# One place fewer for reloaded strips, one more for input strips, and channel sums half a unit earlier

## The chip, the cores and the metric

The kernel runs on one core of one Trainium2 chip. A core has TensorE (PE), VectorE (DVE), ScalarE (ACT), GpSimd (POOL) and SyncE (SP, which here only issues DMAs), an on-chip memory SBUF with 128 partitions, the accumulators in PSUM, and 16 DMA engines to HBM. The metric is the device time of one execution in microseconds (us); lower is better.

## The reference

The input x has 16 images of 112 x 112 pixels with 256 channels in float32. What is computed, cut to what matters:

```python
x  = x + conv3x3_depthwise(sign(groupnorm(x)), sign(kernel))     # x1
v  = groupnorm(x)
gate = sigmoid(fc(mean(v)) + fc(max(v)))                         # per image and channel
xc = v * gate
m, mx = mean(xc, channels), max(xc, channels)                    # two feature maps
y  = state_space_scan(m)                                         # along the pixels, 16 states
s  = conv7x7(concat(m, mx))
x2 = xc * sigmoid(y) + xc * sigmoid(s)
out = x + relu(batchnorm(x2))
```

The channel gate of an image needs the sums of the whole x1 of that image, so the feature maps of an image can only be made once its convolution is done, and the scan and the batch norm need all images.

## The kernel before

The kernel has three stages: (1) a loop over the 16 images that makes x1, the gates and the feature maps; (2) the scan, the 7 x 7 convolution and the sums of the batch norm, with x1 read again; (3) a last pass that reads x1 once more and writes the output. The change is in stage 1 and in the hand-over to stage 2.

**Half steps.** An image is cut into 7 units of 8 rows in each half of the image, and a unit into its two groups of 128 channels. One pair (unit, group) is a half step, h = 0 to 13. In half step h of image i TensorE convolves (18 matmuls with `taps`, L1338), turns, from half step 2 on, two tiles of the next image from pixels to channels on the partitions (`turn_tile`, L1244, 7 transposes each, the first in the midst of the convolution, the second at the end of the half step; the last four of the 28 tiles follow half step 13), and works on two strips of the image before: `channel_sums` (L1277, 16 matmuls, the sum over the channels of a gated strip) and `blocks_back` (L1291, 7 transposes of the maximum over the two channel groups). ScalarE brings turned tiles to SBUF (`evacuate`, L750), converts the convolution (`pack`, L758), brings the channel sums to SBUF (`average`, L813), squares (`square`, L766), and gates a strip (`apply_gate`, L795 and L799: both channel groups for the strips 0, 1 and 10 to 13; for strips 2 to 9 only the first, and VectorE does the second in `gate_half`, L1107). VectorE makes the signs (L961, L976), takes the maximum of the two groups (`max_halves`, L1117), reduces the turned blocks (L1128), and adds the convolution to x (`add_convolution`, L1022, L1028).

**Strips.** The feature maps of image i - 1 are made while image i is convolved. Its x1 is read back from HBM in 14 strips of 896 pixels. `strip_at(i, h, lag)` gives the strip that is `lag` half steps behind: in half step h, SP loads strip h - 1 (`load_g`, L576 to L585), ScalarE gates strip h - 3, VectorE takes the maximum of strip h - 4, TensorE sums and turns back strip h - 5, and ScalarE averages strip h - 5. Below zero these are the last strips of the image before that. Strip 9 of image i - 1 would fall to half step 0 of the next image; it is handled at the end of image i instead: `blocks_back(i - 1, 9)`, a wait for all tiles of the next image, `channel_sums(i - 1, 9)`, and only then `group_sums` (L1250), the matmul on whose result the mean of the next image (L951) and all its signs wait.

**Places.** Reloaded strips go round a ring of four places `xg` (the halves of the two tiles `xc`); `load_g` waits until the strip four before has been summed and its maximum taken. Input strips x go round three places `xin` in `stage`; each load (L569) waits until the tiles of the strip three before have been turned. Sums over channels stand in PSUM in `turn[c % 2]`, the two accumulators that the convolution also uses in turn, so the convolution of half step h waits (`averaged`, L1334) until the sum that was made in the other use of its accumulator has been brought out.

**Averaged sums.** ScalarE writes two strips each into a row buffer `srow[s % 2]`, s = c // 2, and SP stores the pair to HBM (`sums_out`, L594). An image has seven pairs, so its last pair (s = 6) and the first pair of the next image (s = 0) use the same buffer, and `average` of strip 0 waits until the store of pair 6 has landed:

```python
def average(i, c):
    s, b = c // 2, c // 2 % 2
    act.wait_ge(summed, i * NP + c + 1)
    if c % 2 == 0:
        act.wait_ge(sum_out[b], i * (16 * turns(b, 2, NS)) + 16 * (s // 2) + 1)
```

**SP's order.** SP issues everything from one queue, in the order written. In half step h: the next x strip, the store of x1 of half step h - 1 (L589), `load_g` of strip h - 1, then in even half steps `sums_out` of the pair of strip h - 6 (pair 6 in half step 4), then the row of maxima (L599). A wait in one of them holds all that follow.

Before image 0 its x strips are loaded and turned (L569, L1244); then 42 tiny loads of parameters follow on SP (L612, L615), a store of `bands`, and then the first three x strips of image 1. In image 15 there is no next image; TensorE computes part of the 7 x 7 convolution (`spatial`, L556) in its place, for which SP loads features (L440) in half step 3.

Of the kernel before, what the change touches and what calls it, by code (L numbers as in the profile page):

```python
# [5 lines left out]
def binary_conv_then_gated_ssm_block(  # L6
# [74 lines left out]
    with ctx:  # L81
# [6 lines left out]
        def sem(name):  # L88
# [8 lines left out]
        xin = [stage[:, b * SP:(b + 1) * SP].rearrange("p (t c) -> p t c", c=C) for b in range(3)]  # L97
        picks = stage[0:12, 3 * SP:3 * SP + 4 * P]
# [3 lines left out]
            "p (j n) -> p j n", j=NJ) for b in range(4)]  # L102
# [133 lines left out]
        x_in = [sem(f"x_in{b}") for b in range(3)]  # L236
# [30 lines left out]
        g_in = [sem(f"g_in{b}") for b in range(4)]  # L267
# [17 lines left out]
        def sum_ps(c):  # L285

            return turn[c % 2][:, 0:SQ]
# [7 lines left out]
        def ring(i, c):  # L295
            return (i * NP + c) % 4

        def ring_turns(i, c):

            return (i * NP + c) // 4 + 1  # L300
# [262 lines left out]
        with nc.Block() as block:  # L563
            @block.sync
            def _(sp):
                def load_x(i, k):
                    p = pair(k)
                    p0, p1 = unit_px(p // 2, p % 2)
                    sp.dma_start(xin[k % 3], x_strips[i, p0:p1, :].rearrange("(p t) c -> p t c", t=TG)  # L569
                                 ).then_inc(x_in[k % 3], 16)  # L570

                def load_next_x(i, k):
                    sp.wait_ge(turned, i * NTILE + 2 * (k - 3) + 2)
                    load_x(i, k)

                def load_g(i, c):  # L576
# [63 lines left out]
                def image(i):  # L640
                    more = i + 1 < NB
                    if more:
                        sp.wait_ge(turned, i * NTILE + NTILE)
                        for p in range(3):
# [90 lines left out]
            def _(act):  # L735
# [48 lines left out]
                def apply_gate(i, c, resident=False):  # L784
# [4 lines left out]
                    if resident:  # L789
                        act.wait_ge(maxed, i * NP + c - 3)  # L790
                        act.wait_ge(summed, i * NP + c - 3)
# [26 lines left out]
                def image(i):  # L818
                    first, more, channels = i == 0, i + 1 < NB, i >= 1
                    for h in range(NP):  # L820
# [8 lines left out]
                        if (at := strip_at(i, h, 5)) and h >= 1:  # L829
# [21 lines left out]
                    if more and channels:  # L851
                        average(i - 1, 9)
# [10 lines left out]
                average(NB - 2, 9)  # L863
# [356 lines left out]
            def _(pe):  # L1220
                pe.wait_ge(consts_made, 14)

                def turn_tile(i, n):
# [3 lines left out]
                    b = k % 3  # L1227
                    if j == 0:
                        pe.wait_ge(x_in[b], i * (16 * turns(b, 3, NP)) + 16 * (k // 3 + 1))
# [641 lines left out]
```

## Time and profile before

| what | value |
|---|---|
| median of 3 runs | 3481.12 us (3471.48 to 3544.35) |
| the profiled execution | 3476.38 us |
| its span in the trace | 3474.7 us |
| mean granted TensorE clock, as a share of full speed | 0.832 |
| busy: PE, DVE, ACT, POOL | 2596.4, 3053.3, 2693.6, 19.9 us |
| DMA traffic | 1227.99 MB, 353 GB/s over the span |

Stage 1 runs to about 1775 us after the span's start (the last convolution matmul starts at 1772.6 us), stage 2 to about 2485 us, the last pass to the end. All times below are from the start of the span. An arrow in a row names what ended the idle time before the instruction.

### The profile page before, as it was taken

What the parts mean: (1) busy time and instruction counts of PE and PEld (TensorE: products, weight loads), DVE (VectorE), ACT (ScalarE), POOL (GpSimd) and SP (SyncE); (2) the same over time, 40 slices, a digit from 0 to 9 for tenths busy, and PEclk for the clock granted to TensorE, in tenths of its full rate; (3) what the DMA queues carried; (4) which work ended last, traced back from release to release, by engine and by line L of the source; (5) the groups of instructions that cost most, each with busy time, mean ns of one, the idle gap of its engine ahead of it and who ended that gap; (6) DMA issues with size and microseconds to landing.
All of it is one profiled execution on the core that took longest, in us unless ns stands there. A gap on an engine that the chain in (4) does not pass through costs nothing. (4 is left out here: it accounts for less than half of the span.)

```text
span 3474.7 us, 50996 instructions
## 1 busy us (share of the span) xinstructions
PE 2596.4 (75%) x17105; PEld 1661.0 (48%) x17105; DVE 3053.3 (88%) x4395; ACT 2693.6 (78%) x3748; POOL 19.9 (1%) x23
## 2 busy tenths in 40 slices
PE   4899999999999998999877333333377767777676
PEld 3565555655556555566443010000255555555555
DVE  5689989999999998999886599999898899899997
ACT  3788887878888888888674287777788888888887
POOL 1000000000000000000000000000000000000000
PEclk8999999999999999999998555555577787777777
DMA  5898888988889888898765399999499999999998
GB/s 177 316 406 346 352 340 355 396 343 351 350 353 404 350 347 344 350 405 346 254 205 133 87 414 416 416 416 414 198 423 427 427 418 418 419 419 421 420 421 340
DMA packets 258888, 1227.99 MB, mean 353 GB/s; under 512 B 36421, under 2 KB 45537, under 8 KB 244353
## 3 DMA queue, kind: packets, MB, share of 16 engines
q1 hardware_dynamic: 258688, 1225.40, 89.0%
q8 instruction: 117, 1.92, 0.2%
q14 instruction: 83, 0.67, 0.1%
HBM read 805.14 MB, written 420.17 MB: 353 GB/s over the span
## 5 line engine op out<-in xcount | busy, mean ns | idle before, releaser
L1338 PE MATMUL psum<-signs,taps 128*128 128x448 f16 x4032 | 876.6, 362 | 49.1 <-DVE signs L976 44.9
L1759 PE MATMUL psum<-ident,xt 128*128 128x128 f32 x3136 | 560.5, 348 | 281.0 <-ACT stage L1793 232.5
L1759 PEld LDWEIGHTS psum<-ident,xt 128*128 128x128 f32 x3136 | 498.7, 212 | 367.2 <-ACT stage L1793 309.2
L1439 PE MATMUL psum<-signs,picked 12*128 12x448 bf16 x896 | 328.8, 510 | 356.1 <-DMA signs<-gate_scratch 287.3
L1338 PEld LDWEIGHTS psum<-signs,taps 128*128 128x128 f16 x4032 | 395.3, 100 | 381.0 <-issue 48.1
L1793 ACT ACTIVATE stage<-psum 128x512 f32<-128x512 f32 x784 | 407.1, 612 | 173.7 <-DMA out_dram<-stage 149.4
L1814 DVE SCALAR_TENSOR_TENSOR xc<-xt,curs,psum 128x1792 f32<-128x1792 f32 x224 | 456.1, 2077 | 85.7 <-PE psum L1439 81.2
L750 ACT ACTIVATE xt<-psum 128x896 f32<-128x896 f32 x416 | 377.9, 912 | 162.9 <-PE psum L1244 162.7
L1623 DVE SCALAR_TENSOR_TENSOR xc<-xt,curs,psum 128x1792 f32<-128x1792 f32 x224 | 455.6, 2078 | 49.5 <-PE psum L1439 34.4
L1244 PE MATMUL psum<-ident,stage 128*128 128x128 f32 x3136 | 416.5, 277 | 76.6 <-DMA stage<-x_dram 43.7
L1561 ACT ACTIVATE xc<-xc 128x1792 f32<-128x1792 f32 x224 | 380.1, 1697 | 113.6 <-DVE xc L1623 113.6
L1829 DVE TENSOR_TENSOR xt<-xc,xt 128x1792 f32<-128x1792 f32 x224 | 442.6, 2018 | 0.0
L1028 DVE CUSTOM_DVE_ANT_0 xt<-scratch,xt 128x896 f32<-128x896 int8 (+1 forms) x416 | 436.1, 1085 | 0.0
L1244 PEld LDWEIGHTS psum<-ident,stage 128*128 128x128 f32 x3136 | 364.9, 143 | 118.7 <-DMA stage<-x_dram 50.2
L1781 ACT ACTIVATE xc<-xc,bn,curs 128x1792 f32<-128x1792 f32 x224 | 411.3, 1900 | 8.6 <-DVE xc L1814 8.4
L766 ACT ACTIVATE hsum<-xt,nmean 128x1792 bf16<-128x1792 f32 x208 | 370.4, 1781 | 0.7
L1439 PEld LDWEIGHTS psum<-signs,picked 12*128 12x128 bf16 x896 | 86.7, 117 | 562.5 <-DVE xc L1623 380.1
L1128 DVE TENSOR_REDUCE pmax<-psum 128x4 f32<-128x512 f32 x448 | 257.7, 617 | 73.3 <-PE psum L1291 73.2
L758 ACT ACTIVATE scratch<-psum,border 128x896 int16<-128x896 f32 x224 | 223.9, 1000 | 82.8 <-PE psum L1338 82.4
L1117 DVE TENSOR_TENSOR stage<-xc 128x896 f32<-128x896 f32 x224 | 243.9, 1089 | 27.4 <-ACT xc L795 19.5
L976 DVE SCALAR_TENSOR_TENSOR signs<-xt,mean,signs 128x896 f16<-128x896 f32 x208 | 240.3, 1155 | 7.4
L1291 PE MATMUL psum<-ident,stage 128*128 128x128 f32 x1568 | 223.8, 282 | 24.1 <-ACT pmax_rows L806 13.8
(199 smaller groups left out, 2205.9 us busy)
## 6 DMA issues: line engine op xcount, KB each, us to landing
xt<-x_scratch SPq DMA_DIRECT2D x210, 1792.0 KB
stage<-x_dram SPq DMA_DIRECT2D x224, 896.0 KB, 9.0
out_dram<-stage SPq DMA_DIRECT2D x112, 1792.0 KB, 13.7
xc<-x_scratch SPq DMA_DIRECT2D x210, 896.0 KB, 8.3
x_scratch<-xt SPq DMA_DIRECT2D x208, 896.0 KB, 7.5
x_scratch<-last_unit SPq DMA_DIRECT2D x16, 896.0 KB, 6.9
signs<-ssm_scratch SPq DMA_DIRECT2D x28, 448.0 KB, 4.6
signs<-gate_scratch SPq DMA_DIRECT2D x217, 10.5 KB
```

What stands on the lines that cost most here:

```text
L750: nc.scalar.activation(dst, src, ACT.Identity, scale=PACK if part else 1.0, accum_out=xsum_p[:, j, 2 * u + part:2 * u + part + 1]).then_in ...
L1028: nc.vector.tensor_tensor_reduce(out=px, in0=conv, in1=px, scale=1.0 / PACK if part else 1.0, scalar=-3.0e38, op0=ALU.add, op1=ALU.max, ac ...
L1244: ins = nc.tensor.transpose(ring[:, t * P:(t + 1) * P], xin[b][:, t, j * P:(j + 1) * P], ident[:, :])
L1338: return nc.tensor.matmul(turn[h % 2][:, b * 512:b * 512 + HB], taps[:, j, t, :], signs[:, j, r:r + RT // 2, dw:dw + W], start=t == 0, sto ...
L1439: last = nc.tensor.matmul(dst[:, b, :], picked[:, b * P:(b + 1) * P], gate_rows[:, s * BW:(s + 1) * BW], start=True, stop=True)
L1561: nc.scalar.activation(u, u, ACT.Square, accum_out=g2_p[:, n, j, bass.ds(it, 1)]).then_inc(squared3, 1)
L1623: nc.vector.scalar_tensor_tensor(fours(xc[n % 2][:, j, :]), fours(slots[s][:, j, :]), curs[:, h, j:j + 1], gate_ps3[n % 2], ALU.add, ALU.mult,
L1759: last = nc.tensor.transpose(out_ps[k % 4][:, v * C + j * P:v * C + (j + 1) * P], block_in, ident[:, :])
L1781: nc.scalar.activation(u, u, ACT.Relu, bias=bn[:, 7, j:j + 1], scale=curs[:, h, NJ + j:NJ + j + 1]).then_inc(relu_made, 1)
L1793: nc.scalar.activation(outs[n % 2][:, 2 * k:2 * k + 2, :].rearrange("p t c -> p (t c)"), out_ps[k % 4], ACT.Identity).then_inc(staged, 1)
L1814: nc.vector.scalar_tensor_tensor(fours(xc[n % 2][:, j, :]), fours(slots[s][:, j, :]), curs[:, h, j:j + 1], gate_ps4, ALU.add, ALU.mult).th ...
L1829: nc.vector.tensor_tensor(x1, u, x1, ALU.add).then_inc(x2_made, 1)
```

## The change

It does the following:

- The ring `xg` has three places instead of four; `load_g` waits for the strip three before.
- The free place becomes a fourth place of `xin`. An x load waits for the turn of the strip four before, and each strip is loaded one half step earlier: strip 0 of the next image in half step 13 of the image before (for image 1: right behind the x loads of image 0 and ahead of the parameter loads), strips 1 to 3 at the start of an image.
- `channel_sums` and `average` go from five half steps behind to four. `blocks_back` stays at five. The half step 0 now has sums (of strip 10), the special case at the end of an image keeps only `blocks_back(i - 1, 9)`, and `sum_ps` changes its parity so that the sums still lie in the accumulator that is not being convolved into.
- The convolution's wait for `averaged` and the wait of the third last turned tile are moved by one strip to match.
- The call of `sums_out` in SP's program is as before.

```diff
         def sum_ps(c):
-            return turn[c % 2][:, 0:SQ]
+            return turn[(c + 1) % 2][:, 0:SQ]
...
                 def load_x(i, k):
...
+                    b = (i * NP + k) % NX
...
                 def load_next_x(i, k):
-                    sp.wait_ge(turned, i * NTILE + 2 * (k - 3) + 2)
+                    sp.wait_ge(turned, i * NTILE + 2 * (k - NX) + 2)
...
-                    if i * NP + c >= 4:
-                        sp.wait_ge(maxed, i * NP + c - 3)
-                        sp.wait_ge(summed, i * NP + c - 3)
+                    if i * NP + c >= 3:
+                        sp.wait_ge(maxed, i * NP + c - 2)
+                        sp.wait_ge(summed, i * NP + c - 2)
...
-                for p in range(3, NP):
+                for p in range(NX, NP):
                     load_next_x(0, p)
+                load_next_x(1, 0)
...
                     if more:
-                        sp.wait_ge(turned, i * NTILE + NTILE)
-                        for p in range(3):
-                            load_x(i + 1, p)
+                        for p in range(1, NX):
+                            load_next_x(i + 1, p)
                     for h in range(NP):
-                        if h >= 3 and more:
-                            load_next_x(i + 1, h)
+                        if h >= NX - 1 and more and (i + 2 < NB or h < NP - 1):
+                            load_next_x(i + 1 + (h + 1) // NP, (h + 1) % NP)
...
-                        if (at := strip_at(i, h, 5)) and h >= 1:
+                        if at := strip_at(i, h, 4):
                             average(*at)
...
-                        if strip_at(i, h, 6):
-                            pe.wait_ge(averaged, (i - 1) * NP + h - 5)
+                        if strip_at(i, h, 5):
+                            pe.wait_ge(averaged, (i - 1) * NP + h - 4)
...
-                        if (at := strip_at(i, h, 5)) and h >= 1:
+                        if at := strip_at(i, h, 4):
                             pe.wait_ge(unpack_in, i * NP + h)
                             channel_sums(*at)
+                        if (at := strip_at(i, h, 5)) and h >= 1:
                             blocks_back(*at)
...
                             blocks_back(i - 1, 9)
-                            pe.wait_ge(evacuated, (i + 2) * NTILE)
-                            channel_sums(i - 1, 9)
                         group_sums(i + 1)
```

## Rows read from the trace of the kernel before

**Rows 1.** The page, the chain that ended last, share of the span by line
```profile
DMA out_dram<-stage 20%; ACT stage L1793 3%; PE psum L1759 2%; DVE xc L1814 1%; DVE xt L1829 1%; PE psum L1439 0%; ACTq L1792 0%; ACT xc L1781 0%; SPq L1722 0%; ACTq L1712 0%; ACTq L1779 0%; ACTq L1790 0%; ACTq L1798 0%; DVEq L1812 0%; DVEq L1810 0%
```
**Rows 2.** Windows: window, us, busy (instructions) of each engine, clock, DMA share, GB/s
```profile
918.10:1024.90 106.80, 99.20 (x789) 63.83 (x788) 98.61 (x203) 88.77 (x139) 0.00 (x0) 0.98 0.92 362
```
**Rows 3.** Timeline of PE, one image, half steps 3 to 5: start, us, instruction
```profile
1043.50 0.96 PE L1277 MATMUL psum<-xc,over_c 128*32 128x224 f32 x16
...
1050.78 0.96 PE L1277 MATMUL psum<-xc,over_c 128*32 128x224 f32 x16
...
1053.37 2.07 PE L1338 MATMUL psum<-signs,taps 128*128 128x448 f16 x10
...
1060.38 0.55 PE L1291 MATMUL psum<-ident,stage 128*128 128x128 f32 x3 [1.06 <-ACT pmax_rows L806]
```
**Rows 4.** Timeline of ACT, same stretch
```profile
1043.19 1.12 ACT L799 ACTIVATE xc<-xc,gbias,cur 128x896 f32<-128x896 f32 x1
...
1050.07 1.12 ACT L799 ACTIVATE xc<-xc,gbias,cur 128x896 f32<-128x896 f32 x1
...
1052.88 0.35 ACT L813 ACTIVATE hsum<-psum 128x224 f32<-128x224 f32 x1
...
1060.51 0.36 ACT L813 ACTIVATE hsum<-psum 128x224 f32<-128x224 f32 x1 [0.18 <-DMA feat_scratch<-hsum]
```
**Rows 5.** Timeline of DVE, half step 4: the maximum of strip 0
```profile
1054.63 1.09 DVE L1117 TENSOR_TENSOR stage<-xc 128x896 f32<-128x896 f32 x1
```
**Rows 6.** Timeline of SP's DMA issues, half step 4
```profile
1053.64 0.49 SPq L584 DMA_DIRECT2D xc<-x_scratch  x1
1054.18 0.91 SPq L594 DMA_DIRECT2D feat_scratch<-hsum  x1
```
**Rows 7.** The same store one image later, its waiter, and all DMAs of that tensor
```profile
1161.55 0.90 SPq L594 DMA_DIRECT2D feat_scratch<-hsum  x1
...
1169.54 0.36 ACT L813 ACTIVATE hsum<-psum 128x224 f32<-128x224 f32 x1 [1.51 <-DMA feat_scratch<-hsum]
...
DMA to landing us min/median/max: 3.5/6.1/9.6
```
**Rows 8.** Timeline of PE in image 0, from half step 2 on
```profile
87.23 1.75 PE L1244 MATMUL psum<-ident,stage 128*128 128x128 f32 x7 [11.72 <-DMA stage<-x_dram]
...
95.03 0.93 PE L1244 MATMUL psum<-ident,stage 128*128 128x128 f32 x7
...
99.99 0.27 PE L1244 MATMUL psum<-ident,stage 128*128 128x128 f32 x1
```
**Rows 9.** Waits of PE from 200 to 2000 us, and timelines at two image ends
```profile
PE psum L1244 <- DMA stage<-x_dram: 18.8, 12, 2.4
...
683.39 2.46 PE L1244 MATMUL psum<-ident,stage 128*128 128x128 f32 x21
...
692.80 0.16 DVE L951 TENSOR_SCALAR mean<-psum 128x2 f32<-128x2 f32 x1 [0.47 <-PE psum L1250]
...
1223.48 2.46 PE L1244 MATMUL psum<-ident,stage 128*128 128x128 f32 x21
...
1231.21 0.16 DVE L951 TENSOR_SCALAR mean<-psum 128x2 f32<-128x2 f32 x1 [0.96 <-PE psum L1250]
```
**Rows 10.** Timeline of SP's DMA issues before image 0
```profile
48.92 7.03 SPq L612 DMA_DIRECT2D scol<-A_dram  x8
...
78.84 3.02 SPq L569 DMA_DIRECT2D stage<-x_dram  x3
```
**Rows 11.** PE's sums in half step 10, DVE's gating of the strip in half step 9
```profile
985.70 0.96 PE L1277 MATMUL psum<-xc,over_c 128*32 128x224 f32 x16
...
986.12 0.75 DVE L1107 TENSOR_SCALAR xc<-xc,cur,gbias 128x896 f32<-128x896 f32 x1
```
**Rows 12.** Image 15: the feature loads on SP, and PE's wait for them
```profile
1694.12 3.15 SPq L440 DMA_DIRECT2D stage<-feat_scratch  x2
...
1705.04 4.79 PE L556 MATMUL psum<-stage 112*112 112x448 f32 x6 [4.46 <-DMA stage<-feat_scratch]
```

More of the change, by code:

```diff
@@ L97, in binary_conv_then_gated_ssm_block @@
         xin = [stage[:, b * SP:(b + 1) * SP].rearrange("p (t c) -> p t c", c=C) for b in range(3)]
+        NX = 4
         picks = stage[0:12, 3 * SP:3 * SP + 4 * P]
@@ L101, in binary_conv_then_gated_ssm_block @@
         xg = [xc[b // 2][:, :, :].rearrange("p j n -> p (j n)")[:, b % 2 * SP:(b % 2 + 1) * SP].rearrange(
-            "p (j n) -> p j n", j=NJ) for b in range(4)]
+            "p (j n) -> p j n", j=NJ) for b in range(3)]
+        xin.append(xc[1][:, :, :].rearrange("p j n -> p (j n)")[:, SP:2 * SP].rearrange("p (t c) -> p t c", c=C))
         bands0 = xc[0][0:H, :, :].rearrange("p j n -> p (j n)")[:, 0:KS * 2 * H].rearrange(
@@ L235, in binary_conv_then_gated_ssm_block @@
         taps_made = sem("taps_made")
-        x_in = [sem(f"x_in{b}") for b in range(3)]
+        x_in = [sem(f"x_in{b}") for b in range(NX)]
         turned = sem("turned")
@@ L266, in binary_conv_then_gated_ssm_block @@
         gate_in = sem("gate_in")
-        g_in = [sem(f"g_in{b}") for b in range(4)]
+        g_in = [sem(f"g_in{b}") for b in range(3)]
         gated = sem("gated")
@@ L295, in ring @@
         def ring(i, c):
-            return (i * NP + c) % 4
+            return (i * NP + c) % 3
         def ring_turns(i, c):
-            return (i * NP + c) // 4 + 1
+            return (i * NP + c) // 3 + 1
         def tile(n):
@@ L603, in _ @@
                     sp.dma_start(dst[:], src).then_inc(params_in, 16)
-                for p in range(3):
+                for p in range(NX):
                     load_x(0, p)
                 sp.dma_start(lsa[:, :], lsa_d.broadcast_to([H, KS * KS * 2])).then_inc(lsa_in, 16)
-                for p in range(3, NP):
+                for p in range(NX, NP):
                     load_next_x(0, p)
+                load_next_x(1, 0)
                 for src, col in ((A_d[0, :], 0), (B_w_d[:, 0], 1), (B_b_d, 2), (C_w_d[:, 0], 3), (C_b_d, 4)):
@@ L789, in apply_gate @@
                     if resident:
-                        act.wait_ge(maxed, i * NP + c - 3)
-                        act.wait_ge(summed, i * NP + c - 3)
+                        act.wait_ge(maxed, i * NP + c - 2)
+                        act.wait_ge(summed, i * NP + c - 2)
                     else:
@@ L850, in image @@
                     square(i, NU - 1, 1, first)
-                    if more and channels:
-                        average(i - 1, 9)
                     inverse_deviation(i)
@@ L862, in _ @@
                 apply_gate(NB - 2, 11)
-                average(NB - 2, 9)
                 gate_exp(NB - 1)
@@ L1226, in turn_tile @@
                     k = (2 * u + part + 2) % NP
-                    b = k % 3
+                    b = (i * NP + k) % NX
                     if j == 0:
-                        pe.wait_ge(x_in[b], i * (16 * turns(b, 3, NP)) + 16 * (k // 3 + 1))
+                        pe.wait_ge(x_in[b], 16 * ((i * NP + k) // NX + 1))
                     if i == 0:
@@ L1236, in turn_tile @@
                         if i >= 2:
-                            pe.wait_ge(averaged, (i - 2) * NP + 9)
+                            pe.wait_ge(averaged, (i - 2) * NP + 10)
                     elif n >= NTILE - 2:
@@ L1393, in _ @@
                 hidden(NB - 1)
-                channels_late(NB - 2, 9)
+                blocks_back(NB - 2, 9)
                 gate(NB - 1)
```

5 lines of the change are left out of this document (2 added, 3 removed).

## The prediction

> **What bounds the kernel now.** I read the page's chain first. The end of the span is a last pass whose time is DMA stores [rows 1]; its length doesn't depend on stage 1, so what stage 1 gains or loses passes to the end in full. Next the windows, one for each image: an image of stage 1 takes about 107 us, in which TensorE is busy for 99.2, VectorE for 98.6 and the DMA engines for 0.92 of the time [rows 2]. No engine has room; a wait of a microsecond anywhere is likely to be seen, fourteen times over. So I read the timelines of one image, engine by engine, to see who sets the pace where. From mean to half step 2 it is VectorE; from there on TensorE, with ScalarE close behind it in half steps 2 to 5, where it gates both channel groups and still has its two tiles and its squares.
>
> **The change, part by part.** All times are those of the image in [rows 3 to 6]; "old" is the trace, "new" my walk through the new order.
>
> *Sums one half step nearer to the gating.* In half step 3 TensorE comes to its sums at 1043.50 [rows 3]. Before, that was strip 12, gated long ago. Now it is strip 13, whose second gating ends at 1043.19 + 1.12 = 1044.3 [rows 4]: 0.9 late. The blocks, the second tile and ScalarE's move of it follow, so ScalarE's next gating (strip 0) ends not at 1050.07 + 1.12 = 1051.2 but at 1052.1, and the sums of strip 0 in half step 4 start at 1052.2 instead of 1050.78 [rows 3, 4]: 1.4 late. By itself this costs about 1.4 us an image; in the later half steps the gating ends some tenths before the sums. Half step 10 is the other tight one: sums at 985.70, VectorE's gating of that strip ends at 986.12 + 0.75 = 986.9 [rows 11], 1.2 late. VectorE doesn't wait for TensorE in between, so this is not added to the 1.4 but covered by it.
>
> *The average of strip 0.* This is the large term. `average` of strip 0 may not write its row buffer before the store of the last pair of the image before has landed. Old, that store was issued at 1054.18 in half step 4 [rows 6], and the average came one half step later: it started at 1060.51, after a wait of 0.18 us for just this store [rows 4]. One image on it is 1161.55 and 1169.54, with a wait of 1.51 [rows 7]. So landing takes 6.3 to 8.0 us where ScalarE waited, and there was no slack to give away. New, the average stands in half step 4, where ScalarE comes to it at about the old 1052.88 + 1 = 1053.8 [rows 4], while SP still issues the store in half step 4. And SP comes to it later than before: ahead of it in the queue stands `load_g` of strip 3, which with three places waits for the maximum of strip 0 (four places: of the last strip of the image before). That maximum ends at 1054.63 + 1.09 = 1055.7 [rows 5]. Load and store are 0.54 us apart [rows 6], so the store is issued at 1056.3 and, with 6.4 us, lands at 1062.7. ScalarE stands still for 8.9 us, and all that is queued behind it there: a tile, the squares, the gating of strip 1. TensorE's convolution of half step 5 needs the accumulator that holds the sum, so it starts at 1063.2 instead of 1053.37 [rows 3]: 9.8 late.
>
> *TensorE's clock.* It then has idled for 8 us. The nearest row is image 0: after 11.72 us of idle time seven transposes took 1.75 us instead of 0.93, the half rate, and from there to the same place of the next half step it took 95.03 - 87.23 = 7.8 us where the next one takes 99.99 - 95.03 = 5.0 [rows 8]. I take 2.8 us. Back goes the wait of 1.06 us for the row of maxima in half step 5 [rows 3], since ScalarE will have done that row while TensorE is slow. Sum: 9.8 + 2.8 - 1.0 = 11.6 us an image, the 1.4 included (it runs beside the wait for the store). VectorE is held about as long, since its maximum of strip 1 waits for the gating behind the average; so the tight place in half step 10 stays covered. From below: the shortest landing of that tensor is 3.5 us [rows 7], and with no slow clock ScalarE's own order sets the restart, about 7 us. From above: 8.0 us of landing gives 13.2, the longest landing, 9.6, gives 14.8.
>
> It holds for images 2 to 14, 13 x 11.6 = 151 us. In image 1 strip 0 is the first of all and nothing is waited for; 0.9 for the gating. In image 15 the store waits in the same way; the feature loads behind `load_g` in half step 3 come some 3 us later than 1694.12, but TensorE, which idled 4.46 us for them [rows 12], now idles for the average instead. There the slow clock is already in the old time, and half step 10 costs its 1.2 again, since TensorE is slower than VectorE there: about 10.4. Stage 2 begins with a reload that waits for strip 10 instead of 9; I put it at nothing within 2 us.
>
> *The image's end.* The sums of strip 9 stood ahead of the group sums; without their 0.9 us the mean comes 0.5 us earlier (ScalarE's last tile and VectorE's sum of it are then what is late), 14 x 0.5 = 7. The fourth x place brings the last x strip one half step earlier, so the waits for it go: 12 waits, 18.8 us [rows 9]. Not all of it was paid: from the start of the last tiles to the mean it takes 1231.21 - 1223.48 = 7.7 us where there was no such wait, and 692.80 - 683.39 = 9.4 with one of 2.4 [rows 9]. ScalarE, which moves the tiles one by one, hid 0.7 to 0.9 of each. 18.8 - 12 x 0.9 = 8. Together -15 us.
>
> *The start.* Strip 0 of image 1 was loaded behind 42 parameter loads that occupy SP from 48.92 on, at 78.84 [rows 10], and TensorE idled 11.72 us until 87.23 [rows 8]. Now it stands ahead of them, and half step 2 runs without a wait. Half step 3 then waits for strip 1, still behind the parameters. These start earlier by as much as the fourth place speeds up the loads of image 0, which I put at 6 us (3 to 9: one strip is there at the start, and four transfers are under way instead of three). So x is issued near 73 and lands 8.4 us later (87.23 - 78.84), at 81.3; with TensorE slow again for 2.8 us that is like 84.1 at full rate, against 95.03: -11 us (-5 to -13).
>
> The sum: 151 + 10.4 + 0.9 - 15 - 11 = +136. The profiled execution took 3476.4 us (1.7 outside its span), so 3612; the median of the runs is 5 us above it, less than what I can tell.
>
> A rule of the Trainium skill speaks to the largest term. DMA: Bandwidth & Descriptors, section Anatomy of one DMA, gives a transfer a fixed part of about 2 us, most of it the confirmation of the write, and these stores have 7 KB each. By that the store would have landed 2 us after its issue, the old trace would show no wait, and the sum would be near 3550 (an estimate from that page's figure). The trace doesn't agree where it counts: 6.3 and 8.0 us [rows 4, 6, 7], right behind a reload of 896 KB.
>
> **The rivals.**
>
> *The store lands soon.* The landings of that tensor go down to 3.5 us [rows 7]. In the new order TensorE is held up each time, so the DMA engines may have less before the store. Against it: the reload issued 0.54 us ahead of it is the same. With 3.5 us and little of the slow clock, 7 us an image: 13 x 7 + 5.8 + 0.9 - 26 = +72, 3548.
>
> *It lands late.* 9.6 us [rows 7] gives 14.8 an image: 13 x 14.8 + 13.6 + 0.9 - 26 = +181, 3657.
>
> *Not slower: the average isn't held.* This is so if the store has landed before 1053.8, thus was issued by 1047.5, that is in half step 3, ahead of the load of strip 3. What speaks for it is that its data, the average of strip 13, is ready at 1046.4. Against it is the order of SP's program. Then an image pays only 1.4: 13 x 1.4 + 0.9 + 4.6 (image 15: 3.4 for the features behind `load_g`, and half step 10) - 26 = -2, 3474. The same holds if the fourth x place is what counts and I have misread the wait.
>
> **How the numbers follow.** The forecast, landing in 6 to 8 us, has 0.62; soon 0.17; late 0.11; not held 0.10. The likeliest gives 3612. The range leaves out the case "not held" and the tail of "late": 3540 to 3650. A measurement of this kernel can tell about 2%, 70 us. The not-held case and half of the soon case lie within it, 0.18; slower by more 0.81; faster by more 0.01, since all that is gained is 26 us.
>
> **What would show it right or wrong.** Right: in images 2 to 15 ScalarE waits some 8 to 9 us ahead of L813 in half step 4, ended by the store to `feat_scratch`, 14 times, where it was 0.2 and 1.5 us in the rows shown; SP issues that store just behind a reload that waited for VectorE's maximum; L1338 waits 8 us for L813, with slow matmuls behind it; an image takes near 117 us; no PE wait for x at an image's end; TensorE's wait in image 0 shorter and one half step later. Wrong: if the wait at L813 is under 4 us (landing), or absent and images still near 107 us. If images are longer than 120 us, the reload's longer wait also starves a gating, which I hold unlikely: it is issued 2 us later than before and has two half steps, 13 us, to land.

## The result, and the profile after

The changed kernel takes 3627.4 us (median of four runs, 3602.5 to 3652.1) where the kernel before takes 3476.3 in the same comparison: ratio 1.044, 95% interval 1.037 to 1.051. It is slower, as forecast; 3612 had been predicted, with a range of 3540 to 3650. Two of the four runs took 3602 and 3604 us, the other two 3650 and 3652. The profiled execution is one of the longer two: it took 3650.3, its span is 3648.6.

First the sum of waits. The page's group of the convolution and two rows of the waits, from 200 to 2100 us (engine, line, releaser: us in total, times, longest):

```profile
L1338 PE MATMUL psum<-signs,taps 128*128 128x448 f16 x4032 | 900.7, 369 | 172.2 <-ACT hsum L816 129.1
```
```profile
ACT hsum L816 <- DMA feat_scratch<-hsum: 120.8, 15, 13.7
PE psum L1338 <- ACT hsum L816: 128.9, 28, 12.6
```

L816 is `average`. ScalarE stood before it for 120.8 us in all, until a store of the sums had landed: 7.5 to 9.5 us in each of the images 2 to 14, 13.7 in image 15 and 0.5 once behind it. TensorE stood before its convolution for 128.9 us, until ScalarE had made that average. Then one image, the one with its mean at 1066.29, in half steps 3 to 5. SP's DMA issues (to hold against [rows 6]), VectorE's maximum [rows 5], ScalarE [rows 4] and TensorE [rows 3]:

```profile
1104.16 0.55 SPq L592 DMA_DIRECT2D x_scratch<-xt  x1
1107.07 0.37 SPq L587 DMA_DIRECT2D xc<-x_scratch  x1
1107.48 0.73 SPq L597 DMA_DIRECT2D feat_scratch<-hsum  x1
```
```profile
1105.85 1.09 DVE L1117 TENSOR_TENSOR stage<-xc 128x896 f32<-128x896 f32 x1
```
```profile
1102.42 1.12 ACT L802 ACTIVATE xc<-xc,gbias,cur 128x896 f32<-128x896 f32 x1
...
1114.84 0.36 ACT L816 ACTIVATE hsum<-psum 128x224 f32<-128x224 f32 x1 [9.51 <-DMA feat_scratch<-hsum]
```
```profile
1095.67 0.96 PE L1277 MATMUL psum<-xc,over_c 128*32 128x224 f32 x16 [0.89 <-ACT xc L802]
...
1103.68 0.96 PE L1277 MATMUL psum<-xc,over_c 128*32 128x224 f32 x16 [1.17 <-ACT xc L802]
...
1115.34 3.89 PE L1338 MATMUL psum<-signs,taps 128*128 128x448 f16 x10 [9.01 <-ACT hsum L816]
1119.03 1.50 PE L1244 MATMUL psum<-ident,xc 128*128 128x128 f32 x7
...
1122.09 0.96 PE L1277 MATMUL psum<-xc,over_c 128*32 128x224 f32 x16
```

Read them in this order. The maximum of strip 0 ends at 1105.85 + 1.09 = 1106.94; at 1107.07 SP issues the reload of strip 3, which has waited for it; at 1107.48 the store of the last pair follows, which has been behind the reload. It lands near 1114.8, 7.4 us later (the longest of thirteen; 6.1 on average). ScalarE came to the average at 1114.84 - 9.51 = 1105.3, before the store was even issued. TensorE restarts at 1115.34.

Windows of the same image round the stall (us, busy and instructions of PE, PEld, DVE, ACT, POOL, then the granted clock, DMA share, GB/s):

```profile
1098.00:1106.00 8.00, 6.83 (x57) 4.51 (x56) 7.93 (x15) 6.62 (x9) 0.00 (x0) 1.00 0.93 340
1106.00:1115.00 9.00, 0.33 (x3) 0.09 (x1) 6.09 (x11) 0.16 (x1) 0.00 (x0) 0.72 1.01 388
1115.00:1119.00 4.00, 3.66 (x10) 1.56 (x11) 0.00 (x0) 4.00 (x7) 0.00 (x0) 0.50 0.58 237
1119.00:1127.00 8.00, 8.00 (x62) 5.67 (x61) 4.34 (x7) 5.47 (x9) 0.00 (x0) 0.92 0.32 110
```

TensorE is all but idle for 9 us; the granted clock falls to 0.50 (1.2 GHz), stays there for the first 4 us of the restart and comes back. In the same 9 us the DMA engines are busy all the time (1.01, 388 GB/s), so the store lands beside full traffic. Ten matmuls take 3.89 us instead of 2.07 [rows 3].

From the times of L951, the mean that begins each image, of L1338 and of the first matmul of the second stage (L1439 before, L1438 after) the whole can be added up:

| | before | after | difference |
|---|---|---|---|
| mean of image 0 | 60.96 | 53.47 | -7.5 |
| mean of image 2 | 259.24 | 242.82 | -16.4 |
| an image, 2 to 14 (13 intervals) | 108.01 | 117.74 | +9.73 |
| mean of image 15 | 1663.34 | 1773.50 | +110.2 |
| last convolution matmuls of image 15 | 1771.24 | 1891.26 | +120.0 |
| second stage's first matmul | 1981.99 | 2112.64 | +130.7 |

The last pass, on which nothing was changed, took 43 us longer in this execution. Profiled once more (e12 below), the changed kernel has a last pass as long as before. So about 131 us of the difference between the two traces belong to the change.

### The profile page after: what moved, and what is told of

It reads as the page before. It is cut to its first block and busy times, and to the rows that moved or that the text cites. A ratio compares the mean times of both kernels' runs of the same rounds, so it can differ in the third digit from the quotient of the medians.

```text
span 3648.6 us, 50997 instructions
## 1 busy us (share of the span) xinstructions
PE 2637.4 (72%) x17105; PEld 1684.1 (46%) x17105; DVE 3058.9 (84%) x4395; ACT 2695.9 (74%) x3748; POOL 19.7 (1%) x23
## 5 line engine op out<-in xcount | busy, mean ns | idle before, releaser
L1338 PE MATMUL psum<-signs,taps 128*128 128x448 f16 x4032 | 900.7, 369 | 172.2 <-ACT hsum L816 129.1
L1758 PE MATMUL psum<-ident,xt 128*128 128x128 f32 x3136 | 572.5, 354 | 307.6 <-ACT stage L1792 265.0
L1758 PEld LDWEIGHTS psum<-ident,xt 128*128 128x128 f32 x3136 | 508.0, 212 | 395.9 <-ACT stage L1792 332.8
L1338 PEld LDWEIGHTS psum<-signs,taps 128*128 128x128 f16 x4032 | 402.6, 101 | 518.3 <-issue 200.4
L1438 PE MATMUL psum<-signs,picked 12*128 12x448 bf16 x896 | 333.0, 516 | 357.2 <-DMA signs<-gate_scratch 290.6
L1117 DVE TENSOR_TENSOR stage<-xc 128x896 f32<-128x896 f32 x224 | 243.9, 1089 | 130.1 <-ACT xc L802 95.8
L1438 PEld LDWEIGHTS psum<-signs,picked 12*128 12x128 bf16 x896 | 87.8, 118 | 566.8 <-DVE xc L1622 380.5
L1244 PE MATMUL psum<-ident,stage 128*128 128x128 f32 x2352 | 309.5, 275 | 35.5 <-POOL counts L722 17.5
L1244 PEld LDWEIGHTS psum<-ident,stage 128*128 128x128 f32 x2352 | 272.1, 142 | 67.3 <-POOL counts L722 17.5
L1277 PE MATMUL psum<-xc,over_c 128*32 128x224 f32 x3584 | 218.7, 362 | 36.5 <-ACT xc L802 26.7
## 6 DMA issues: line engine op xcount, KB each, us to landing
out_dram<-stage SPq DMA_DIRECT2D x112, 1792.0 KB, 13.7
```

What stands on the lines that cost most here:

```text
L1244: ins = nc.tensor.transpose(ring[:, t * P:(t + 1) * P], xin[b][:, t, j * P:(j + 1) * P], ident[:, :])
L1338: return nc.tensor.matmul(turn[h % 2][:, b * 512:b * 512 + HB], taps[:, j, t, :], signs[:, j, r:r + RT // 2, dw:dw + W], start=t == 0, sto ...
L1438: last = nc.tensor.matmul(dst[:, b, :], picked[:, b * P:(b + 1) * P], gate_rows[:, s * BW:(s + 1) * BW], start=True, stop=True)
L1758: last = nc.tensor.transpose(out_ps[k % 4][:, v * C + j * P:v * C + (j + 1) * P], block_in, ident[:, :])
```

## The experiments

The medians of e1 to e12 stand against runs of the kernel before on the same chip as each, 3471 to 3473 us in each set; the row "changed" is the first result, against 3476. "Start" is the time from the mean of image 0 to that of image 2, "image" the average of images 2 to 14, "hand-over" the time from the last convolution to the second stage, all from each kernel's own trace.

| kernel | us | ratio, 95% | start | image | image 15 | hand-over |
|---|---|---|---|---|---|---|
| before | 3472 | | 198.3 | 108.0 | 107.9 | 210.8 |
| changed | 3627 | 1.044 (1.037 to 1.051) | 189.4 | 117.7 | 117.8 | 221.4 |
| e1, store half a step earlier | 3485 | 1.004 (1.003 to 1.006) | 189.9 | 109.2 | 110.8 | 216.5 |
| e2, store ahead of the reload | 3567 | 1.028 (1.026 to 1.030) | 188.2 | 114.9 | 115.1 | 218.5 |
| e3, row buffers in turn | 3482 | 1.003 (1.002 to 1.004) | 189.3 | 109.0 | 113.3 | 215.8 |
| e4, sums only | 3584 | 1.033 (1.031 to 1.034) | 195.3 | 116.1 | 115.9 | 212.7 |
| e5, places only | 3580 | 1.031 (1.029 to 1.033) | 190.5 | 115.4 | 117.7 | 230.0 |
| e6, places, buffers in turn | 3491 | 1.009 (1.005 to 1.012) | 189.0 | 108.6 | 112.2 | 229.0 |
| e7, other start, buffers in turn | 3461 | 0.997 (0.996 to 0.998) | 184.6 | 107.9 | 108.1 | 212.0 |
| e8, sums, buffers in turn | 3490 | 1.006 (1.004 to 1.007) | 196.9 | 109.0 | 109.9 | 212.9 |
| e9, stores on GpSimd | 3485 | 1.004 (1.001 to 1.008) | 190.2 | 109.0 | 113.9 | 219.1 |
| e10, other start, GpSimd | 3461 | 0.998 (0.994 to 1.002) | 184.2 | 108.0 | 108.9 | 213.3 |
| e11, one strip ahead | 3474 | 1.002 (0.999 to 1.004) | 197.5 | 107.6 | 108.4 | 211.4 |
| e12, changed again | 3612 | 1.040 (1.038 to 1.043) | 189.8 | 118.1 | 118.2 | 218.7 |

**Is it the wait for the store?** Two kernels take it away in different ways. e1 moves the store:

```diff
-                        if h % 2 == 0 and (at := strip_at(i, h, 6)):
+                        if h % 2 and (at := strip_at(i, h, 5)):
                             sums_out(at[0], at[1] // 2)
```

(Cut; the stores behind the last image are shifted to match.)

> The changed kernel, with one thing moved: SP issues the store of a pair of sums in the half step in which its second average is made (odd half steps), not one later, so the store of the last pair goes out in half step 3, ahead of the reload of strip 3. Theory (the changed kernel loses its time because the average of strip 0 waits for that store): the store is issued near 1098 to 1099 in the image that has its mean at 1066.3, lands 7 us later, near the time at which ScalarE comes to the average (1105.3); the wait of 9.5 us falls under 1.5, an image takes 108 to 109 us instead of 117.7, and the total is 3465 to 3485. Rival (three places for the reloaded strips hold SP, and the late reloads hold the gating, whatever the store does): an image stays above 114 us, the total above 3560. Rival (the sums one half step nearer are what costs, since TensorE waits for the gating): about the same as the rival before in the total, but with the wait of L1338 at channel sums in half steps 3 and 4, not at its convolution.

Measured: 3484.9, an image 109.2. The image with its mean at 1007.3, SP and ScalarE:

```profile
1041.88 0.37 SPq L587 DMA_DIRECT2D xc<-x_scratch  x1
1042.30 0.58 SPq L597 DMA_DIRECT2D feat_scratch<-hsum  x1
```
```profile
1046.91 0.36 ACT L816 ACTIVATE hsum<-psum 128x224 f32<-128x224 f32 x1 [0.57 <-DMA feat_scratch<-hsum]
```

The store goes out 35.0 us after the mean instead of 41.2 (1107.48 - 1066.29) and the wait is 0.57 us; over images 2 to 14 it is 0.3 to 1.8 us. In image 15 ScalarE still waits 6.9 us. e3 leaves SP alone and separates the buffers, so that the last pair of an image and the first of the next no longer share one:

```diff
-                    s, b = c // 2, c // 2 % 2
+                    s, b = c // 2, (i * NS + c // 2) % 2
...
-                                 srow[s % 2][0:P:32, :, :]).then_inc(sum_out[s % 2], 16)
+                                 srow[(i * NS + s) % 2][0:P:32, :, :]).then_inc(sum_out[(i * NS + s) % 2], 16)
```

(Cut; the waits that count these stores are changed to match.)

> The changed kernel, in which the two row buffers of the averages are taken in turn through all images (buffer by the count of all pairs, not by the count within an image), so the last pair of an image and the first of the next no longer share one. SP's order stays. Theory (wait for the store in flight): no wait of ScalarE for the store of the sums; image 108 to 109 us, total 3460 to 3480, within 8 us of the kernel in which the store is issued a half step earlier. Rival (the place of the store in SP's queue matters by itself, as it is held behind the reload of strip 3): the total stays above 3560.

Measured: 3482.1, an image 109.0, 2.8 us from e1. The wait lists of e3 show what is left of it at `average`:

```profile
L816 ACT ACTIVATE hsum<-psum x224: 333/355/362, 173.7 to 1860.2; 128x224 f32<-128x224 f32 x112
...
  DMA feat_scratch<-hsum: 0.2, 1
```

0.2 us instead of 120.8, and 8.8 us of each image are gone (117.7 - 109.0). It takes two things to make the stall: the shared buffer (e3 has the late store and no stall) and the late issue (e1 has the shared buffer and nearly no stall). e1 ends at the upper end of what was expected, e3 2 us above it: they are still 10 to 13 us slower than before, in spite of a start that is shorter. Of that the images hold 1.0 to 1.1 us each, image 15 another 3 to 5 and the hand-over 5 to 6; the next kernels show where they come from. In image 15 of e3 TensorE waits 7.5 us for the features of the 7 x 7 convolution, where the kernel before waited 4.46 [rows 12]: its load stands on SP behind a reload that now has a place to wait for, and is issued 34.5 us after the mean instead of 30.8.

**Which part of the change makes it?** The two halves of the diff, each alone on the kernel before. e4 has the moved sums and averages (the hunks of `sum_ps`, `average`, `channel_sums` and their waits), e5 has all the others.

> The kernel before with only one part of the change: the channel sums and the average one half step nearer to the gating; four places for reloaded strips and three for x as before. Theory: SP issues the store of the last pair near the old time (1054.2, right behind a reload that waits for nothing new) and it lands 6.4 to 8 us later; ScalarE comes to the average at 1053.8 and waits 6.8 to 8 us; the restart of the convolution is 7.7 late, with 2.8 for the slow clock, less 1.0 and less 0.5 at the image's end: +9.0 an image, 14 of them, +126, so about 3602 (3570 to 3620). Rival (it takes the ring of three as well, because only the reload of strip 3 that waits for a maximum makes the store late): within 15 us of the kernel before, 3465 to 3490.

> The kernel before with only the other part: three places for the reloaded strips, four for x, strip 0 of image 1 loaded ahead of the parameters; sums and averages where they were. Theory: the start gains 14 to 17 us, the image's end 0.5 us each (8 in all); the store of the last pair goes out 2 us later than before (behind the reload that waits for the maximum of strip 0) and the average of half step 5 waits some 2 us for it, of which TensorE sees 0 to 1: total 3450 to 3475. Rival (three places starve the gating): images above 110 us, total above 3500.

e4 measured 3583.8: the theory holds, though with 116.1 an image is 0.9 us shorter than it said. Four places don't help, as the store is still issued in half step 4, 39 us after the mean, where the kernel before issues it. ScalarE's waits for it are 6.1 to 7.5 us in images 2 to 14.

e5 is a miss: 3580.5 against 3450 to 3475. The time is the rival's (images above 110, total above 3500), but no gating in the images waits for a reload; this is what stands in it (SP, ScalarE, TensorE):

```profile
1095.65 0.37 SPq L587 DMA_DIRECT2D xc<-x_scratch  x1
1096.06 0.58 SPq L597 DMA_DIRECT2D feat_scratch<-hsum  x1
```
```profile
1102.13 0.36 ACT L816 ACTIVATE hsum<-psum 128x224 f32<-128x224 f32 x1 [5.00 <-DMA feat_scratch<-hsum]
```
```profile
1094.57 0.96 PE L1280 MATMUL psum<-xc,over_c 128*32 128x224 f32 x16
...
1102.63 3.89 PE L1341 MATMUL psum<-signs,taps 128*128 128x448 f16 x10 [4.14 <-ACT hsum L816]
```

`load_g` waits not only for the maximum of the strip three back but also for its sums. With the sums where they were, those of strip 0 come in half step 5 (1094.57 + 0.96 = 1095.5), so SP issues the reload and the store behind it a whole half step late, and the average, which also comes in half step 5, waits 5 us for it. So either half of the change makes this stall on its own, in a different half step: e4 brings the average to the store, e5 the store to the average.

**The same two halves with the stall taken away.** e6 is e5, e8 is e4, each with e3's edit.

> The kernel with only the other places (three for reloaded strips, four for x, sums where they were), which took 115.4 us for an image, now with the two row buffers taken in turn through all images, so no average waits for the store of the last pair. In that kernel the reload of strip 3 waits in half step 4 for the sums of strip 0, which are made in half step 5, and holds the store behind it. Theory (the held store is all that costs): image 108.0 to 108.5, total 3455 to 3475, start 16 us earlier. Rival (SP held for half a step each time makes the reloads and x strips themselves late for ScalarE and TensorE): image above 111, total above 3500.

> The kernel before with the sums one half step nearer to the gating (four and three places as before) and the two row buffers taken in turn through all images. It prices the move of the sums alone. Theory (the three waits of TensorE for the second gating in half steps 3 to 5 and the wait for the sum of x cost 1.0 us an image, 3 us more in image 15; the three places cost nothing in the images): image 109.0, total 3484 to 3492. Rival (the 1.0 us comes from the three places, for instance by reloads landing later): image 108.0, total 3468 to 3476.

e6: an image is 108.6, so the stall was indeed the cost in e5's images, but the total is 3490.8, 16 us above the expectation. It is the hand-over that was forgotten: 229.0 against 210.8. At its place in the tail ScalarE waits for the reload of strip 13 (L798, `apply_gate`):

```profile
1789.06 1.14 ACT L798 ACTIVATE xc<-xc,gbias,cur 128x896 f32<-128x896 f32 x1 [2.85 <-DMA xc<-x_scratch]
...
1800.63 1.13 ACT L798 ACTIVATE xc<-xc,gbias,cur 128x896 f32<-128x896 f32 x1 [9.17 <-DMA xc<-x_scratch]
```

In the kernel before there is no such wait. With three places the last reloads wait for sums that are made only after the last image, at the end of a chain of small steps.

e8: 3489.8 and 109.0 an image, both as expected. So the move of the sums costs 1.0 us an image net, and e3, which has the places as well, takes the same 109.0. Both list the same waits of TensorE: the sums for the second gating (e3's rows)

```profile
PE psum L1277 <- ACT xc L802: 35.3, 40, 1.7
PE psum L1250 <- DVE xsum L945: 19.3, 14, 1.6
```

and, at an image's end, the group sums for VectorE's sum of x. In neither is there a wait for x at the image's end any more, and e8 has only three x places: the sums that left the end are enough to remove it. In e6, which has the fourth place and the sums of strip 9 still at the end, the waits for x are down to 1.5 us in all, but TensorE now waits there for ScalarE's move of the last tiles, 28.1 us in 14 waits against 7.9 in 13 in the kernel before (e6's row, then the row before):

```profile
PE psum L1280 <- ACT xt L753: 28.1, 14, 2.5
```
```profile
PE psum L1277 <- ACT xt L750: 7.9, 13, 0.9
```

ScalarE converts the convolution (`pack`) fourteen times an image. The starts of these, counted from the mean and averaged over images 2 to 14, show where an image gains and loses:

| kernel | 6th | 11th | 12th | 14th | next mean | 14th to mean |
|---|---|---|---|---|---|---|
| before | 43.8 | 78.2 | 85.0 | 98.5 | 108.0 | 9.5 |
| changed | 54.0 | 88.5 | 95.8 | 109.3 | 117.7 | 8.4 |
| e3 | 45.5 | 79.9 | 87.0 | 100.6 | 109.0 | 8.4 |
| e8 | 45.5 | 79.9 | 87.0 | 100.6 | 109.0 | 8.4 |
| e6 | 44.0 | 78.3 | 85.1 | 98.6 | 108.6 | 10.0 |

With no stall the moved sums cost 1.7 us by the 6th and 0.4 more by the 14th, most of it in half step 10, 2.1 in all, and give back 1.1 at the image's end. The fourth place alone (e6) makes the end 0.5 longer, not shorter.

**The landing.** e2 swaps two calls in one half step, so that the store no longer waits behind the reload:

```diff
-                        if at := strip_at(i, h, 1):
-                            load_g(*at)
                         if h % 2 == 0 and (at := strip_at(i, h, 6)):
                             sums_out(at[0], at[1] // 2)
+                        if at := strip_at(i, h, 1):
+                            load_g(*at)
```

> The changed kernel, with the store of the sums put ahead of the reload in the same half step of SP's program. SP then issues it about 2.6 us earlier (near 38.6 us after the mean instead of 41.2), since it no longer waits behind the reload that waits for the maximum of strip 0, and no reload of 896 KB stands right ahead of it. Theory (the landing takes 6 to 7.5 us whatever stands right ahead): the wait of ScalarE falls from 8.2 to about 5.6 us, an image takes 115 us, the total is near 3567 (3550 to 3580). Rival (the reload ahead is what makes the landing long, and alone it lands in 2 to 3.5 us): wait under 2 us, image 110 to 111 us, total 3490 to 3505.

```profile
1083.67 0.57 SPq L597 DMA_DIRECT2D feat_scratch<-hsum  x1
1086.00 0.37 SPq L587 DMA_DIRECT2D xc<-x_scratch  x1
```
```profile
1089.49 0.36 ACT L816 ACTIVATE hsum<-psum 128x224 f32<-128x224 f32 x1 [5.24 <-DMA feat_scratch<-hsum]
```

Measured: 3566.9, an image 114.9; in the image shown a wait of 5.24, and the store lands 1089.49 - 1083.67 = 5.8 us after its issue. Worked out in the same way for images 2 to 14, landing takes 6.0 us on average in e2 (5.6 to 7.2), 6.1 in the changed kernel (5.4 to 7.4) and 6.5 when that was profiled again (e12, 5.9 to 8.0), 6.5 in e4 (6.1 to 7.5). So the reload right ahead adds nothing to the landing that can be seen; what e2 gains is the earlier issue, 38.4 us after the mean instead of 41.2. The shares of the DMA engines over an image are 0.85 to 0.89 in the changed kernel, e2 and e4, and 1.0 while the stores shown are under way. The Trainium skill gives a DMA that GpSimd issues a fixed part of about 2 us (DMA: Bandwidth & Descriptors, Anatomy of one DMA). The traces don't agree that such a store has landed by then: SP's stores took 5.4 us and more where ScalarE waited for them in images 2 to 14, and in e9, where GpSimd issues them, the shortest of them landed in 1.7 us but the median in 5.2.

**Is it SP's queue?** e9 gives the stores of the sums to GpSimd, which has nothing else to do in the images:

```diff
+                for i in range(NB - 2):
+                    for s in range(NS):
+                        if (i, s) != (NB - 3, NS - 1):
+                            sums_from(pool, i, s)
                 pool.wait_ge(turned, NB * NTILE)
...
```

(Cut; the stores behind the images go to GpSimd too, and their semaphores count from 0 instead of 1.)

> The changed kernel, with all stores of the channel sums issued by GpSimd, which has no other work in the images, instead of by SP; buffers, places and sums stay as changed. GpSimd waits for the second average of a pair and nothing else, so the store of the last pair goes out in half step 3, not behind the reload of strip 3. Theory (the order in one queue makes the wait): it has landed before ScalarE comes to the average of strip 0, waits there under 1.5 us, image 109 us, total 3475 to 3485. Rival (a store from GpSimd is issued or lands 3 us or more later than one from SP): waits of 2 to 5 us, image 110 to 113, total 3500 to 3540.

```profile
1038.73 0.79 POOL L567 DMA_DIRECT2D feat_scratch<-hsum  x1 [14.62 <-ACT hsum L818]
```
```profile
1038.08 0.35 ACT L818 ACTIVATE hsum<-psum 128x224 f32<-128x224 f32 x1
1045.81 0.35 ACT L818 ACTIVATE hsum<-psum 128x224 f32<-128x224 f32 x1
```

Measured: 3484.7, image 109.0, both in the range expected. The store is issued 0.3 us after the end of the average that it carries (1038.08 + 0.35), and the next image's average, 7.7 us later, finds it landed. Buffers, ring and sums are as in the changed kernel; what differs is the queue, and with it the time of the issue.

**The start, and a version that beats both.** e7 keeps places and sums of the kernel before, takes the row buffers in turn, and loads three x strips of image 1 ahead of the 42 parameter loads, which are issued two at a time in images 0 and 1. e10 is the same start with the stores on GpSimd instead. e11 has only one strip ahead:

```diff
+                sp.wait_ge(turned, NTILE)
+                load_x(1, 0)
                 for src, col in ((A_d[0, :], 0), (B_w_d[:, 0], 1), (B_b_d, 2), (C_w_d[:, 0], 3), (C_b_d, 4)):
```

> The kernel before with its places and sums as they were; the three x strips of image 1 are loaded ahead of the 42 parameter loads, which are issued two at a time in the half steps of images 0 and 1, and the two row buffers are taken in turn. Theory (TensorE's 11.72 us without work in image 0 came from SP's queue alone): the start is 14 to 25 us shorter at the mean of image 2, images 108.0, nothing else moves: 3448 to 3460. Rival (the start is bound by the x loads themselves, about 400 GB/s, not by the queue): under 6 us gained, 3466 to 3474.

> The kernel before (places, sums and row buffers as they were), the three x strips of image 1 ahead of the parameter loads and these two at a time in the half steps of images 0 and 1, and the stores of the channel sums on GpSimd. Theory (the queue of SP was all that the start and the small waits for that store needed): as the kernel with the same start and the buffers in turn, which took 3461: 3455 to 3465, images 107.9. Rival (GpSimd's stores disturb VectorE, or land later): images above 108.5, total above 3470.

> The kernel before with x strip 0 of image 1 alone ahead of the 42 parameter loads; three places for x. Theory (the changed kernel's 16 us at the start come mostly from the fourth place, with which the loads of image 0 and so the parameters start 6 us earlier; a strip alone only moves TensorE's wait to half step 3, where strip 1 is issued near 80 us and lands 8.4 us later): 3 to 6 us gained at the mean of image 2, total 3464 to 3469. Rival (the one strip ahead is what gains): 12 to 16 us, total 3455 to 3460.

e7 measured 3461.2, 0.997 (0.996 to 0.998), 1 us above its range: the only one whose interval lies below 1. From mean 0 to mean 2 it takes 184.6 us instead of 198.3; 13.7 us gained, 15.6 at the mean of image 2. Its total gains 9.5, as the medians go. It takes the part of the change that was worth having without the places and the sums. e10 is as fast (3460.8), as expected, with an interval that includes 1. e11 gives 0.8 us in that stretch (its mean of image 2 is 5.5 earlier, but 4.7 of that it has at mean 0, on which the edit has no bearing) and nothing in the total (3473.8 where 3464 to 3469 had been expected); TensorE's wait only moves to half step 3:

```profile
90.63 1.76 PE L1246 MATMUL psum<-ident,stage 128*128 128x128 f32 x7 [15.71 <-DMA stage<-x_dram]
```

So one strip ahead of the parameters gains nothing if the next is still behind them and image 0 isn't faster itself. With the fourth place, image 0 has its mean at 53.3 to 53.5 in all eight traces with four x places, and at 56.1 to 61.0 in the six with three; and SP is at the parameters at 42.60 instead of 48.92 [rows 10].

> The changed kernel once more, without any edit, to see what a profile shows that was not taken in one of its longer executions. Theory: images 117.7 us as before, since the wait for the store is the same in each; the last pass takes 990 us as in the kernel before, and the total is near 3603. Rival (the 43 us in the last pass of the first profile come from the change): the last pass takes over 1020 us again, the total is 3640 to 3655.

e12 measured 3611.9 (3608.9 to 3616.7), ratio 1.040, 9 us above what was expected; an image takes 118.1. From the first transposition of the last pass to the end it takes 972.6 us (before: 973.5), where the first profile has 1016.3; so the rival is refuted. Windows of the last pass, first those of the changed kernel's first profile, then e12's:

```profile
3100.00:3648.00 548.00, 375.60 (x1829) 291.17 (x1828) 447.40 (x233) 410.35 (x519) 0.00 (x0) 0.73 0.95 373
```
```profile
3100.00:3607.00 507.00, 351.00 (x1849) 273.97 (x1848) 449.23 (x233) 411.58 (x521) 0.00 (x0) 0.78 0.98 406
```

## Why the prediction was right, step by step

**The average of strip 0**, the largest term, came as described: the store behind the reload, the reload behind the maximum (0.13 us after it), the landing 6.1 us on average where 6.4 was taken, the average held in images 2 to 15, fourteen times. The hold is 8.2 us on average in images 2 to 14 (7.5 to 9.5) where 8.9 was said. e3, e1 and e9 show it causes 8.6 to 8.8 us an image.

**The slow clock** was put at 2.8 us. In the image shown it takes 1122.09 - 1115.34 = 6.75 us from the restart to the sums; a half step earlier (1098.15 to 1103.68, 1.17 of it a wait) 4.4. So 2.4.

**The sum for an image**: 11.6 less 1.1 for the image's end, 10.5 net; measured 9.7. Two errors of opposite sign lie in it, and both are ahead of the end. By the 6th conversion the changed kernel is 10.2 us late and stays at 10.3 until the 11th, where 11.6 had been worked out: the hold is 0.7 shorter and the slow clock takes 0.4 less. In half step 10, which was to stay covered, another 0.5 is lost. The sums by themselves, put at 1.4 us, cost 2.1 (e8): TensorE waits for the gating in three half steps (3, 4 and 5, 0.8 to 1.2 each), and in half step 10. **The image's end** gives 1.1 us as forecast (9.5 to 8.4), but not for the reason that carried half of it. The forecast gave 7 of its 15 us to the sums that leave the end and 8 to the fourth x place. e8 has three x places and gains the same 1.1; e6 has four and its end is 0.5 longer. So the size is right and the share of the fourth place is luck: without the waits for x, TensorE waits 1.4 us (19.3 in 14) for VectorE's sum of x, which the prediction had named as what is late then.

**Image 15**: +9.9 against 10.4, but the hold there is 13.7 us, not 8.9: ScalarE, with no tiles of a next image to bring in, comes to the average 34.2 us after the mean instead of 39.0, and the store lands where it does in the others, 48 us after the mean. The prediction took the same hold as elsewhere.

**The start**: -16.4 at the mean of image 2 against -11, outside -5 to -13. The fourth place brings the mean of image 0 forward by 7.5, of which 2 to 5 are this one trace of the kernel before, the latest of the six with three x places (56.1 to 59.1 in the others); without them the gain at the mean of image 2 is 11.5 to 14.5. And TensorE waits 5.27 us instead of 11.72 in image 0. The mis-sized term is what the fourth place does for image 0 itself, which was counted only through the parameter loads.

**The hand-over** was put at nothing within 2 us; it is +10.6, the one step whose mechanism failed. The prediction saw the reload that now waits for strip 10 instead of 9, but took its wait to cost nothing; strip 10 is only summed behind the last image. This reload, of strip 13, is issued at 1910.66 (19.4 us after the last convolution, where the kernel before issues it 16.7 after), right behind the sums at 1908.81, and makes ScalarE wait 3.27 us:

```profile
1915.48 1.13 ACT L798 ACTIVATE xc<-xc,gbias,cur 128x896 f32<-128x896 f32 x1 [3.27 <-DMA xc<-x_scratch]
```

All eight traces with three places for reloaded strips show such a wait, none of the six with four does, and their hand-over is 5.0 to 19.2 us longer than before's. Four traces with the reloads and sums of this part unchanged (before, e7, e10, e11) take 210.8 to 213.3, the moved sums alone 212.7 and 212.9 (e4, e8); so of the 5.0 and 5.7 in e3 and e1 the wait of 3.1 us is likely the greater part, and the rest is within what such traces differ by. Of the other 5 in the changed kernel the trace shows only this: TensorE's clock was 0.50 from 1925 to 1939, over the first chunks of the scan, where it was 1.00 in the kernel before at the same distance from the last convolution (1805 to 1819). What decides that the clock falls there in one execution and less in another (e12: 1.00 in that stretch, +7.9 for the hand-over) stays open.

The misses nearly cancel: 5 at the start and 11 in the images against 11 in the hand-over, total +131 where +136 was forecast. That the total of 3612 is met so closely (3612 in e12, 3627 in the first four runs) is luck; its terms are not that good.

**The rivals.** "Lands soon" (3548) is refuted: in images 2 to 15 of the changed kernel no landing under 5.4 us. The 3550 that the prediction worked out for a landing of 2 us is nearly the same figure as for 3.5 us; by its own terms 1.5 us less in fourteen images would be near 3530. "Lands late" (3657) had the first profile's time but not its mechanism, since the extra 43 us lie in the last pass. "Not held" needed the store in half step 3, ahead of the reload of strip 3; e1 does just that and comes to 3485 where 3474 had been worked out; the hand-over (5.7) and the sums (2.1 instead of 1.4 an image) are the larger part of the difference.

## What to carry to other kernels

Before a consumer is moved nearer to its producer, look who shares its buffer: a wait of 0.2 us for a store in flight is a deadline met with no slack, and here moving either the waiter (e4) or the issue (e5) by half a step cost 7 to 8 us an image, both 10. In an in-order queue of DMA issues every wait of an entry is also a wait of those behind it; a ring made smaller delays the neighbours in the queue, not only its own loads. A small store belongs on an idle engine's queue or into a buffer that nobody needs soon.

## What the runs showed that was not expected

Landing: a store of 7 KB takes 6 us beside DMA engines that are busy all the time (1.01 and 388 GB/s in the window shown), and it makes no difference that can be seen whether SP has issued 896 KB 0.4 us ahead of it (6.1) or not (6.0).

GpSimd's issue of such a store costs no more than SP's: 0.58 us in the median of 112, as in the changed kernel, and VectorE, which works beside it, is not slower (an image 109.0 in e9 as in e3).

The last pass: in the first profile of the changed kernel its second half moves 373 GB/s where e12 moves 406, with a granted clock of 0.73 where e12 has 0.78; which of the two makes the other was not found.
